# State-space stage on one core: VectorE takes x times dt ahead of two taps and of y's remainder, GpSimd the decayed x ahead of the gate weights' split

## Chip, cores and metric

One core of a Trainium2 chip runs the whole program. The metric is the device time of one execution in microseconds; three executions of the kernel before took 2430.52 to 2433.77 us, median 2432.82.

## What is computed

A network of two layers on 2 sequences of 512 tokens with 512 features: a Mamba2 mixer, a sparse dequantised linear layer, attention, and a gated feed-forward layer, each with a residual and a layer norm. The change lies in the mixer. Cut to what matters (128 heads of 64 channels in 8 groups, a state of 128, chunks of 128 tokens):

```python
xBC = silu(conv(xBC, conv_w, 4 taps) + conv_b)
x, Bm, Cm = split(xBC)
dt = clip(softplus(dt + dt_bias)); dA = dt * A; cs = cumsum(dA)      # per chunk
xdt    = x * dt
Ydiag  = (C B^T * exp(cs_l - cs_s), lower triangle) @ xdt
states = B^T @ (exp(cs_last - cs) * xdt)                              # per chunk
Yoff   = C @ previous_states * exp(cs)
y      = Ydiag + Yoff + x * D
yg     = y * silu(gate)
out    = (yg * rsqrt(mean(yg^2 over the group) + eps) * norm_w) @ out_proj_w.T
```

## The kernel before

The mixer works in 128 slots, one for each tile of 128 channels (two heads) of one sequence: 8 groups (g), in each 2 sequences (b) of 8 tiles (i). Channels lie on partitions and the sequence's 512 tokens in the free dimension, except behind the transposes of x, where tokens of a chunk lie on partitions. Slot n of all engines does these parts of neighbouring tiles, and each engine has its own written-out order of them:

- TensorE (from `scan` to `output`): the scan of tile n (lines 811 and 815, needs the masked E, the decayed C and the silu of the gate), the states of n+1 (lines 59 to 61, need the low half `xwlo` of the decayed x), the projection of x for n+3, that of the gate for n+1, the transposes of x of n+2 (`turn_x`, line 833), in some slots the projections, products or transposes of B and C for the next sequence, and the output projection of n-1. A projection is 12 matmuls of 512 columns: each fp32 operand is split in a leading 16-bit part and a remainder, and three products are summed.
- ScalarE: in every second slot the exps of n+1 and n+2 (line 996), then square and leading part of y (1002, 1005), in the first 8 slots of a group a copy of the output weights' leading part (230), tap 0 of x for n+3 (243), the clips of the decays for n+3 (990), the silu of the gate for n+1 (1009), the silu of x for n+3 (248), which waits for the third tap on VectorE.
- VectorE: u = x D + scan's bank of n (1176), the state recurrence of n+1 (1115, 1120), u times the gate's silu (1181), the mask on E of n+1 (1109), then the taps 1, 2 and 3 of x for n+3 (256) with y's remainder (1199) behind tap 1 and x times dt of n+2 (`turned_x`, 1128, reads the bank of the transposes) behind tap 2. In the first slot of each sequence four additions of the outputs (1148) follow, in two slots three taps of B or C.
- GpSimd: the decayed C of n+1 (`decayed_C`, 1280), the output weights' remainder (226), the sum of squares (1297), the remainders of the next group's weights (209: B, C, then x in slots 7 to 14, then the gate in slots 9 to 16), and the decayed x of n+2 (`decayed_x`: 1285 and its low half 1289), which waits for x times dt.
- SyncE issues the loads in a fixed order, each held by a semaphore: the rows of exp(cs) once the scan is done, those of cs once the clips that used their buffer are done, then weights.

Slots 1 to 16 are the body of a loop that runs 7 times (`slots`, line 676 on), slot 0 stands before it and 15 slots behind it. The slot that ends the body is the first of the next group, so each engine jumps back there six times between two bodies.

Of the kernel before, what the change touches and what calls it, by code (L numbers as in the profile page):

```python
# [33 lines left out]
def lead(words):  # L34

    return words.bitcast(BF16)[..., 1::2]
# [33 lines left out]
def tile_at(g, m):  # L70

    if isinstance(g, int) and not 0 <= 16 * g + m <= LAST_TILE:
        return None
    gg, mm = g + m // 16, m % 16
    return Tile(g * 16 + m, gg, mm // 8, mm % 8, gg * 2 + mm // 8)
# [13 lines left out]
def conv_of_slot(s, kind):  # L89
    if kind == "x":  # L90
        return s.u * 10 + (5 + (s.i if is_last_unit(s) else CONV_X[s.i]))
    return s.u * 10 + (5 + (CONV_B if kind == "B" else CONV_C))
# [20 lines left out]
def ring_bank(b, use):  # L113
    return (b + use) % 2
# [516 lines left out]
def mixer(k, io, sc, aw):  # L631
# [3 lines left out]
    with ExitStack() as tmp:  # L635
# [50 lines left out]
        def of_heads(table, t, c0, c1):  # L686

            return (table[:, CH * t.b + c0:CH * t.b + c1, bass.ds(t.g, 1), 2 * t.i:2 * t.i + 2].squeeze(2)
                    .unsqueeze(3).to_broadcast([P, c1 - c0, 2, HD]))

        def by_head(x):
            return x.rearrange("p c (h d) -> p c h d", d=HD)

        def chan(table, t):

            return table[:, bass.ds(t.g, 1), t.b, t.i:t.i + 1].squeeze(1)
# [5 lines left out]
        def next_unit(s):  # L702

            return None if is_last_unit(s) else Tile(s.u * 8 + 8, s.g + s.b, 1 - s.b, 0, s.u + 1)

        with nc.Block() as block:
# [397 lines left out]
            def _(dve):  # L1104
                def masked(t):
                    dve.wait_ge(exp_done, t.n + 1)
                    dve.wait_ge(cbm_done, t.u + 1)
                    e = E[t.i % 4][:].rearrange("p h c t -> p h (c t)")
                    nc.vector.tensor_tensor(e, e, cbm[t.b][:].rearrange("p c t -> p (c t)").unsqueeze(1).to_broadcast([P, 2, T]),  # L1109
                                            ALU.mult).then_inc(m_done, 1)  # L1110

                def state(t, c):
                    if c == 0:
                        dve.wait_ge(st_ready, t.n + 1)
                        nc.vector.tensor_copy(st[t.i % 2][:, 0], W[:, 0:P]).then_inc(s_step, 1)
                        return
                    dve.wait_ge(s_step, 3 * t.n + c)
                    for h in range(2):
                        r = slice(h * HD, (h + 1) * HD)
                        mm = nc.vector.scalar_tensor_tensor(  # L1120
                            out=st[t.i % 2][:, c, r], in0=st[t.i % 2][:, c - 1, r], scalar=head(sc.cd, t, c, h),
                            in1=W[:, c * P + h * HD:c * P + (h + 1) * HD], op0=ALU.mult, op1=ALU.add)
                    mm.then_inc(s_step, 1)

                def turned_x(t):

                    dve.wait_ge(xt_ready, t.n + 1)
                    nc.vector.tensor_tensor(by_head(xt[t.i % 2][:]), by_head(W[:, :].rearrange("p (c d) -> p c d", d=P)),  # L1128
                                            of_heads(sc.dtt, t, 0, CH), ALU.mult).then_inc(xt_done, 1)
# [11 lines left out]
                def mean_square(units, b):  # L1141
                    dve.wait_ge(ss_ready, units)
                    nc.vector.tensor_scalar(ms[:], bank_SS(units, b)[:, 0:CH], SPREAD ** 2 / GC, EPS * SPREAD ** 2,
                                            ALU.mult, ALU.add).then_inc(ms_done, 1)
# [26 lines left out]
                def slot(g, m):  # L1171
                    s, n1, n2, n3 = (tile_at(g, m + d) for d in range(4))
                    nu = next_unit(s)
                    ended = s.i == 0 and not (isinstance(s.u, int) and s.u == 0)
                    dve.wait_ge(y_ready, s.n + 1)
                    nc.vector.scalar_tensor_tensor(out=u[s.i % 2][:], in0=sc.xc[s.i % 4][:], scalar=chan(sc.D, s), in1=Y[:, :],  # L1176
                                                   op0=ALU.mult, op1=ALU.add).then_inc(y_done, 1)
                    if n1:
                        state(n1, 0)
                    dve.wait_ge(y_done, s.n + 1)  # L1180
                    nc.vector.tensor_tensor(u[s.i % 2][:], u[s.i % 2][:], gz[s.i % 2][:], ALU.mult).then_inc(yg_done, 1)  # L1181
                    if n1:
                        state(n1, 1)
                        state(n1, 2)
                        masked(n1)
                    if ended:
                        mean_square(s.u, s.b)

                    def taps(kind, dst, t, j, behind=(None, None)):
                        q = conv_of_slot(s, kind)  # L1190
                        bank = ring_bank(s.b, x_use(s) if kind == "x" else USE_B if kind == "B" else USE_C)
                        for d in range(1, 4):
                            sc.conv(dve, q, bank, dst, t.g, t.b, j, d)
                            if d < 3 and behind[d - 1]:
                                behind[d - 1]()

                    def remainder():
                        dve.wait_ge(hi_done, s.n + 1)
                        nc.vector.scalar_tensor_tensor(out=ylo[s.i % 2][:], in0=u[s.i % 2][:], scalar=chan(sc.nw, s),
                                                       in1=yhi[s.i % 2][:], op0=ALU.mult, op1=ALU.subtract).then_inc(lo_done, 1)  # L1200

                    if n3:
                        taps("x", sc.xc[n3.i % 4], n3, 2 + n3.i, (remainder, lambda: turned_x(n2)))
                    else:
                        remainder()
                        if n2:
                            turned_x(n2)
                    if nu and s.i == 2:
                        taps("B", sc.xcB, nu, 0)
                    if nu and s.i == 4:  # L1210
                        taps("C", sc.xcC[nu.b], nu, 1)
                    if nu and s.i == 5:
                        masked_CB(nu, ring_bank(s.b, USE_CB))
                    if nu and s.i == 6:
                        rest_of_B(nu, k.bank[ring_bank(s.b, USE_BT)])
                    if ended:
                        for half in range(2):
                            add_output(s.u, 1 - s.b, half)
                    if is_last_unit(s):
                        tail(s)  # L1220
# [54 lines left out]
            def _(pool):  # L1275
# [7 lines left out]
                def decayed_x(t):  # L1283
                    pool.wait_ge(xt_done, t.n + 1)
                    nc.gpsimd.tensor_tensor(by_head(xw[t.i % 2][:]), by_head(xt[t.i % 2][:, 0:CH - 1]), of_heads(sc.wdec, t, 0, CH - 1),  # L1285
                                            ALU.mult).then_inc(xw_done, 1)
                    pool.wait_ge(xw_done, t.n + 1)
                    x = xw[t.i % 2][:]
                    nc.gpsimd.tensor_tensor(xwlo[t.i % 2][:], x, lead(x), ALU.subtract).then_inc(xw_lo, 1)
# [21 lines left out]
                def slot(g, m):  # L1311
                    s, mm = tile_at(g, m), m % 16
                    more = not (isinstance(s.g, int) and s.g == NG - 1)
                    if tile_at(g, m + 1):
                        decayed_C(tile_at(g, m + 1))
                    if mm < XT:
                        sc.split_wo(pool, s.g, mm)
                    accumulate(s)
                    if s.i == 0 and not (isinstance(s.u, int) and s.u == 0):
                        root(s.u)  # L1320
                    if more:
                        if mm == 4:
                            sc.split_bc(pool, s.g + 1, 0)
                        if mm == 6:
                            sc.split_bc(pool, s.g + 1, 1)
                        if 7 <= mm <= 14:
                            sc.split_wx(pool, s.g + 1, mm - 7)
                        if 9 <= mm:
                            sc.split_wz(pool, s.g + 1, mm - 9)
                    if m == 16:  # L1330
                        sc.split_wz(pool, s.g, XT - 1)
                    if tile_at(g, m + 2):
                        decayed_x(tile_at(g, m + 2))
                    if is_last_unit(s):
                        tail(s)

# [1031 lines left out]
```

## Time and profile before

| | before |
|---|---|
| median of 3 runs | 2432.82 us (2430.52 to 2433.77) |
| the profiled execution | 2433.26 us |
| its span, first to last instruction | 2431.4 us |
| mean granted TensorE clock | 0.987 |
| TensorE matmuls busy | 2343.2 us (96%) |
| VectorE busy | 1794.1 us (74%) |
| ScalarE busy | 1584.3 us (65%) |
| GpSimd busy | 1377.3 us (57%) |

Groups are counted from 0, and so are the slots of a group (m). The state-space stage lasts from about 59 us to about 1510 us. Busy shares are means over all stages. A time-ordered row has a start, a duration, the engine, the line and the operation with the tile it writes and those it reads; brackets hold the idle time in front of it and what ended that. "issue" there is time in which the engine waited for nothing that the profile shows.

### The profile page before, as it was taken

Reading aid. Unit: us, or ns where it says so; the run is one execution under the profiler, and the core shown is the slowest. Engines: PE = TensorE matmul, PEld = TensorE weight load, DVE = VectorE, ACT = ScalarE, POOL = GpSimd, SP = SyncE. Lnnn points to the kernel's source line nnn. Section 1 sums busy time; section 2 is a strip of 40 time slices with the busy share of each in tenths; the row PEclk is TensorE's granted clock in tenths of the full one; section 3 lists DMA queues with packets and bytes.
Section 4 is the critical chain, followed back from the end, with each engine's and each line's share of the span. In section 5 each row is a group of like instructions: output and inputs, shape, how many; then the busy total and the mean of one; then the engine's idle time right before and its main releaser. Section 6 shows DMA issues by size and latency. Waiting matters only on the chain. (4 is left out here: it accounts for less than half of the span.)

```text
span 2431.4 us, 49850 instructions
## 1 busy us (share of the span) xinstructions
PE 2343.2 (96%) x16008; PEld 1328.4 (55%) x16008; DVE 1794.1 (74%) x3250; ACT 1584.3 (65%) x3327; POOL 1377.3 (57%) x1178
## 2 busy tenths in 40 slices
PE   6999999999999999999999998879999999999898
PEld 3555555555555555555555554445555556555444
DVE  6777777777777787777777885567787777888613
ACT  6776776776776776776776774355665555655533
POOL 5576576576576576576576579344344434454323
PEclk8999999999999999999999999889999999999999
DMA  7343343343343343343343441320010110100000
GB/s 244 120 134 113 111 136 113 112 137 111 111 137 111 110 136 113 112 137 111 112 137 110 132 152 36 129 89 14 36 40 14 41 36 14 40 10 14 1 1 35
DMA packets 117294, 218.95 MB, mean 90 GB/s; under 512 B 10016, under 2 KB 43424, under 8 KB 115840
## 3 DMA queue, kind: packets, MB, share of 16 engines
q1 hardware_dynamic: 116992, 215.29, 27.0%
q8 instruction: 145, 2.38, 0.4%
q14 instruction: 157, 1.29, 0.2%
HBM read 212.10 MB, written 3.15 MB: 89 GB/s over the span
## 5 line engine op out<-in xcount | busy, mean ns | idle before, releaser
L990 ACT ACTIVATE E<-wq,cst 128x128 f32<-128x128 f32 x1024 | 311.7, 389 | 2.2 <-PEq L298 2.2
L256 DVE SCALAR_TENSOR_TENSOR xc<-bank,taps,xc 128x511 f32<-128x511 f32 (+2 forms) x384 | 283.0, 737 | 24.6 <-ACT xc L243 24.1
L1963 POOL TENSOR_TENSOR qT<-qT,qrot 128x512 f32<-128x512 f32 x64 | 81.3, 1270 | 358.3 <-DVE qrot L1852 358.3
L1297 POOL TENSOR_TENSOR acc<-acc,sq 128x512 f32<-128x512 f32 x112 | 162.6, 1452 | 183.5 <-ACT sq L1002 183.5
L61 PE MATMUL bank<-xhi,wx 128*128 128x512 f16 x640 | 242.7, 379 | 0.0
L60 PE MATMUL bank<-xlo,wx 128*128 128x512 f16 x640 | 242.6, 379 | 0.0
L59 PE MATMUL bank<-xhi,wx 128*128 128x512 f16 x640 | 242.5, 379 | 0.0
L1109 DVE TENSOR_TENSOR E<-E,cbm 128x1024 f32<-128x1024 f32 x128 | 235.0, 1836 | 0.9
L1280 POOL TENSOR_TENSOR ecs<-ecs,xcC 128x768 f32<-128x768 f32 x128 | 235.2, 1837 | 0.4 <-POOLq L298 0.4
L1176 DVE SCALAR_TENSOR_TENSOR u<-xc,D,bank 128x512 f32<-128x512 f32 x128 | 95.7, 747 | 177.1 <-PE bank L815 166.4
L1285 POOL TENSOR_TENSOR xw<-xt,wdec 128x384 f32<-128x384 f32 x128 | 106.5, 832 | 174.5 <-DVE xt L1128 174.4
L811 PE MATMUL bank<-E,xt 128*64 128x128 f32 x2048 | 185.6, 280 | 14.6 <-issue 7.3
L1002 ACT ACTIVATE sq<-u 128x512 f32<-128x512 f32 x112 | 70.5, 629 | 196.8 <-DVE u L1181 195.5
L59 PE MATMUL bank<-xhi,wz 128*128 128x512 f16 x512 | 195.3, 381 | 0.4 <-DVE u L1176 0.3
L60 PE MATMUL bank<-xlo,wz 128*128 128x512 f16 x512 | 195.2, 381 | 0.0
L61 PE MATMUL bank<-xhi,wz 128*128 128x512 f16 x512 | 195.1, 381 | 0.0
L59 PE MATMUL bank<-wohi,yhi 128*128 128x512 bf16 x512 | 194.2, 379 | 0.0
L60 PE MATMUL bank<-wolo,yhi 128*128 128x512 f16 x512 | 194.2, 379 | 0.0
L61 PE MATMUL bank<-wohi,ylo 128*128 128x512 bf16 x512 | 194.2, 379 | 0.0
L1780 ACT ACTIVATE probs<-bank,nmx 128x512 f32<-128x512 f32 (+3 forms) x256 | 131.5, 526 | 67.6 <-DVE nmx L1882 67.6
L811 PEld LDWEIGHTS bank<-E,xt 128*64 128x64 f32 x2048 | 120.2, 137 | 64.6 <-issue 62.1
L209 POOL TENSOR_TENSOR wx<-wx 128x512 f16<-128x512 f32 x80 | 147.7, 1850 | 10.5 <-DMA wx<-in_w_xbc 10.5
(265 smaller groups left out, 6617.3 us busy)
## 6 DMA issues: line engine op xcount, KB each, us to landing
wq<-cs_rows SPq DMA_DIRECT2D x128, 512.0 KB, 4.0
ecs<-ecs_rows SPq DMA_DIRECT2D x128, 384.0 KB, 3.6
wx<-in_w_xbc SPq DMA_DIRECT2D x80, 256.0 KB, 2.6
wz<-in_w_z SPq DMA_DIRECT2D x64, 256.0 KB, 2.6
wo<-in_w_o SPq DMA_DIRECT2D x64, 256.0 KB, 3.9
wq<-in_wq SPq DMA_DIRECT2D x8, 1024.0 KB, 5.6
awo_raw<-in_wo SPq DMA_DIRECT2D x32, 256.0 KB, 3.0
wkv<-in_wkv SPq DMA_DIRECT2D x8, 512.0 KB, 3.7
```

Of the source, the lines that this page charges most:

```text
L59: nc.tensor.matmul(out, lhs[0], rhs[0], start=first, stop=False, skip_group_check=skip)
L60: nc.tensor.matmul(out, lhs[0], rhs[1], start=False, stop=False, skip_group_check=skip)
L61: return nc.tensor.matmul(out, lhs[1], rhs[0], start=False, stop=last, skip_group_check=skip)
L209: self.nc.gpsimd.tensor_tensor(rest(w), w, lead(w), ALU.subtract).then_inc(sem, 1)
L256: self.nc.vector.scalar_tensor_tensor(out=dst[:, d:T], in0=self.k.bank[bank][:, 0:T - d], scalar=self.taps[:, bass.ds(g, 1), b, j, 3 - d:4 ...
L811: mm = nc.tensor.matmul(Y[r, cols], xt[t.i % 2][:, c, r], E[t.i % 4][:, h, c], start=True, stop=c == 0, skip_group_check=True)
L990: ins = nc.scalar.activation(E[t.i % 4][:, h, c], sc.csr[t.i % 2][:, h, c * P:(c + 1) * P], ACT.Relu, scale=-1.0, bias=head(sc.cst, t, c, h))
L1109: nc.vector.tensor_tensor(e, e, cbm[t.b][:].rearrange("p c t -> p (c t)").unsqueeze(1).to_broadcast([P, 2, T]), ALU.mult).then_inc(m_done, 1)
L1280: nc.gpsimd.tensor_tensor(e[:], e[:], sc.xcC[t.b][:, P:T].unsqueeze(1).to_broadcast([P, 2, T - P]), ALU.mult).then_inc(cs_done, 1)
L1285: nc.gpsimd.tensor_tensor(by_head(xw[t.i % 2][:]), by_head(xt[t.i % 2][:, 0:CH - 1]), of_heads(sc.wdec, t, 0, CH - 1), ALU.mult).then_inc( ...
L1297: nc.gpsimd.tensor_tensor(acc[t.b][:], acc[t.b][:], sq[:], ALU.add).then_inc(acc_done, 1)
L1780: ins = nc.scalar.activation(pr[h % 2][:, P_OFF[i]:P_OFF[i] + (i + 1) * P], k.bank[bank][:, at:at + (i + 1) * P], ACT.Exp, bias=nmx[h % 2] ...
```

## The change

Two moves, with no operation added or removed. On VectorE the two pieces behind the taps of x change places: x times dt of tile n+2 comes behind tap 1, y's remainder of tile n behind tap 2. On GpSimd the decayed x of n+2 comes ahead of the split of the next group's gate weights, in slots 9 to 16; in the other slots there is no such split and the order is as before. In the last group GpSimd's order does not change.

```diff
@@ vector, slot
                     if n3:
-                        taps("x", sc.xc[n3.i % 4], n3, 2 + n3.i, (remainder, lambda: turned_x(n2)))
+                        taps("x", sc.xc[n3.i % 4], n3, 2 + n3.i, (lambda: turned_x(n2), remainder))
@@ gpsimd, slot
                             sc.split_bc(pool, s.g + 1, 1)
                         if 7 <= mm <= 14:
                             sc.split_wx(pool, s.g + 1, mm - 7)
-                        if 9 <= mm:
-                            sc.split_wz(pool, s.g + 1, mm - 9)
+                    if tile_at(g, m + 2):
+                        decayed_x(tile_at(g, m + 2))
+                    if more and 9 <= mm:
+                        sc.split_wz(pool, s.g + 1, mm - 9)
                     if m == 16:
                         sc.split_wz(pool, s.g, XT - 1)
-                    if tile_at(g, m + 2):
-                        decayed_x(tile_at(g, m + 2))
```

## Rows read from the trace of the kernel before

**Rows 1.** Busy time of each engine in three stretches, with clock and DMA share

```profile
core 0: us, PE busy (x) PEld busy (x) DVE busy (x) ACT busy (x) POOL busy (x), PEclk, DMA share, GB/s
100.00:1430.00 1330.00, 1325.10 (x9635) 750.59 (x9634) 1028.99 (x1708) 976.45 (x1888) 870.05 (x669) 1.00 0.38 121
...
425.40:447.43 22.03, 21.43 (x163) 11.89 (x161) 17.05 (x32) 15.33 (x32) 12.27 (x12) 1.00 0.27 95
607.63:629.94 22.31, 21.41 (x163) 11.89 (x161) 17.85 (x32) 15.33 (x32) 12.21 (x12) 1.00 0.27 93
```

**Rows 2.** The waits from 100 to 1430 us: total, times, longest

```profile
POOL xw L1285 <- DVE xt L1128: 154.8, 117, 3.8
DVE u L1176 <- PE bank L815: 152.7, 108, 2.9
...
PEld bank L811 <- issue: 47.6, 102, 1.1
...
DVE u L1176 <- issue: 10.6, 6, 2.1
...
PEld bank L59 <- POOL xwlo L1289: 2.0, 6, 0.3
```

**Rows 3.** Time-ordered rows of a plain slot with a gate split, from 408 us

```profile
408.63 0.74 DVE L256 SCALAR_TENSOR_TENSOR xc<-bank,taps,xc 128x511 f32<-128x511 f32 x1
...
409.29 0.86 DVE L1199 SCALAR_TENSOR_TENSOR ylo<-u,nw,yhi 128x512 f16<-128x512 f32 x1
...
409.57 0.60 PE L833 MATMUL bank<-identity,xc 128*128 128x128 f32 x4
409.57 1.49 POOL L209 TENSOR_TENSOR wz<-wz 128x512 f16<-128x512 f32 x1
...
410.08 0.74 DVE L256 SCALAR_TENSOR_TENSOR xc<-bank,taps,xc 128x510 f32<-128x510 f32 x1
...
410.74 0.68 DVE L1128 TENSOR_TENSOR xt<-bank,dtt 128x512 f32<-128x512 f32 x1
...
411.33 0.73 DVE L256 SCALAR_TENSOR_TENSOR xc<-bank,taps,xc 128x509 f32<-128x509 f32 x1
...
411.59 0.83 POOL L1285 TENSOR_TENSOR xw<-xt,wdec 128x384 f32<-128x384 f32 x1 [0.53 <-DVE xt L1128]
...
412.50 0.83 POOL L1289 TENSOR_TENSOR xwlo<-xw 128x384 f16<-128x384 f32 x1
```

**Rows 4.** Time-ordered rows of loop ends, engine by engine

```profile
424.89 2.00 ACT L996 ACTIVATE E<-E 128x1024 f32<-128x1024 f32 x2
...
428.87 0.78 ACT L243 ACTIVATE xc<-bank,taps 128x512 f32<-128x512 f32 x1
...
448.03 2.00 ACT L996 ACTIVATE E<-E 128x1024 f32<-128x1024 f32 x2
...
451.58 0.77 ACT L243 ACTIVATE xc<-bank,taps 128x512 f32<-128x512 f32 x1
...
1158.64 0.77 ACT L243 ACTIVATE xc<-bank,taps 128x512 f32<-128x512 f32 x1
...
430.23 1.05 POOL L209 TENSOR_TENSOR wz<-wz 128x512 f16<-128x512 f32 x1
...
432.21 0.37 SPq L197 DMA_DIRECT2D wq<-cs_rows  x1
...
425.40 0.75 DVE L1176 SCALAR_TENSOR_TENSOR u<-xc,D,bank 128x512 f32<-128x512 f32 x1 [2.49 <-PE bank L815]
...
430.45 1.36 DVE L1199 SCALAR_TENSOR_TENSOR ylo<-u,nw,yhi 128x512 f16<-128x512 f32 x1
...
433.65 2.71 DVE L1148 SCALAR_TENSOR_TENSOR resid<-bank,rstd,resid 128x512 f32<-128x512 f32 x4
438.48 0.75 DVE L1176 SCALAR_TENSOR_TENSOR u<-xc,D,bank 128x512 f32<-128x512 f32 x1 [2.12 <-issue]
...
1154.55 0.75 DVE L1176 SCALAR_TENSOR_TENSOR u<-xc,D,bank 128x512 f32<-128x512 f32 x1 [2.49 <-PE bank L815]
...
1167.73 0.75 DVE L1176 SCALAR_TENSOR_TENSOR u<-xc,D,bank 128x512 f32<-128x512 f32 x1 [1.38 <-issue]
```

**Rows 5.** The gate's silu and the scan behind it in the ninth slot of group 2

```profile
524.89 0.60 ACT L1009 ACTIVATE gz<-bank 128x512 f32<-128x512 f32 x1
...
525.82 0.42 PEld L811 LDWEIGHTS bank<-E,xt 128*64 128x64 f32 x8 [0.42 <-issue]
```

## The prediction

> **What bounds the kernel now.** I read the page's busy shares first, then the stage as one window, then the table of waits of the stage, then a plain slot and a loop end in time order. TensorE is busy 96% of the span, and between 100 and 1430 us, nearly all of the stage that the change touches, 1325 of 1330 us [rows 1]. So a slot lasts as long as its matmuls, and a reordering on VectorE or GpSimd can only give back what is left of TensorE's idle time, or add to it. The table of waits says how little that is: 2.0 us in six waits for the low half of the decayed x, which is exactly what the change hurries, and behind it 47.6 us in 102 pieces ahead of a scan, about 0.42 us each, which stand in plain slots too where nothing is late [rows 2]. GpSimd, on the other hand, waits 154.8 us for VectorE's turned x, and VectorE 152.7 us for the scan's bank [rows 2]. Both are slack, since nobody on TensorE waits for them in a plain slot.
>
> **The plain slot, step by step [rows 3].** Today VectorE runs tap 1 at 408.63, y's remainder at 409.29, tap 2 at 410.08, x times dt at 410.74, tap 3 at 411.33 to 412.06. With the change x times dt stands behind tap 1, which ends at 409.37. TensorE's transposes of that x run only from 409.57 to 410.17. A signal between engines takes about 0.17 us (x times dt ends at 411.42, GpSimd begins at 411.59), so x times dt can begin at about 410.34: 0.40 us earlier than now, after 0.97 us of new waiting. Behind it wait tap 2, the remainder and tap 3, by name.
> Tap 2 then begins 0.60 us later, at 410.94, and the remainder would at 411.60. There it meets the decayed x, which GpSimd begins at 411.19 (the 0.40 earlier) and ends at 412.02. What such a meeting costs is shown at 430.45, where the remainder takes 1.36 us: the split that GpSimd began at 430.23 ends at 431.28, and the remainder 0.53 us behind it; the one at 409.29 took 0.86 [rows 3, 4]. So the remainder ends at about 412.6, the low half, due at 412.1, waits for it and ends at 413.4, against 413.33 now, and tap 3 runs from 412.55 to 413.28: **1.22 us later**. The 0.40 us won on x times dt is given back by the collision. Bounds: without the collision tap 3 is 0.8 us later and the low half 0.4 us earlier; with a remainder that must let the low half go first too (0.83 us), tap 3 is some 2.0 us later.
> The Trainium skill (GPSIMD Engine Reference, Key points) says that GpSimd shares its SBUF interfaces with VectorE and contends with VectorE instructions that have two SBUF inputs; the remainder has two, and the 1.36 us row agrees. Without that rule the low half would be 0.4 us earlier in each plain slot, still with nobody waiting for it.
>
> **GpSimd's half of the change.** In slots 9 to 15 of a group the gate weights' split (1.05 us alone, 1.49 beside the remainder [rows 3, 4]) now runs behind the decayed x. It filled GpSimd's wait for VectorE; that wait becomes longer and the split comes after. No matmul of this group reads it (it is a gate weight of the next one), no load is held on it. What it pushes is the next slot's decayed C, by about 1.1 us, which the scan reads a whole slot later. It costs VectorE up to 0.6 us in the product with the gate, where a short slot follows; in an even slot that product is not what ScalarE waits for, as next shown. I cost it at nothing on TensorE; the cover is that slot's length, and gone it would be the 0.6 us.
>
> **What is late next: ScalarE.** Its silu waits for tap 3, then comes a table load, and in every second slot the pair of exps, the square, and the tap of the next x. At the loop end of group 1 the exps end at 426.89 and the tap begins at 428.87 [rows 4]. Where ScalarE ran without a gap, the tap began 1.55 us behind the exps (450.03 to 451.58 [rows 4]). With tap 3 late by 1.2 the exps end at about 428.1 and the tap begins at 429.65: 0.78 us later. Who waits for it? Two places.
> (a) The ninth slot (m = 8) of a group. The gate's silu ends at 525.49 and the scan begins at 525.82 [rows 5]. Its tap moves by about 0.2 us (no output weight to copy there, 0.6 us less), the silu ends at 525.7, plus 0.12: just inside. Cost 0; if tap 3 is 0.3 us later still, 0.3 in each of 8 slots.
> (b) The loop end. VectorE's last addition ends at 436.36, and its next instruction comes only at 438.48, 2.12 us later, on "issue" [rows 4]; six such gaps make 10.6 us [rows 2]. In that slot pair TensorE is idle for 0.6 us (21.43 busy of 22.03), in group 2's for 0.9 [rows 1]. The restart is 9.61 us behind ScalarE's tap in group 1, and 9.09 in group 5 (1158.64 to 1167.73), while from the last addition it varies more. I read it so: the clips behind the tap release SyncE's row load (432.21), a burst of data follows, and VectorE's code for the next pass comes behind that burst. So the restart moves with the tap. New tap 4.25 us behind the slot's u; today 3.47 in group 1 and 4.09 in group 5 [rows 4]; of the six, two are like the first and four between. Shifts 0.78 and 0.16, mean about 0.45, times 6: **+2.7 us**. Bounds: 0 (the restart has its own time), 0.78 x 6 = 4.7.
> Advanced Engine Details and Errata of the Trainium skill (Control Flow Timing) gives a taken branch about 51 ns. The 2.12 us row says otherwise here; by the page VectorE would restart with the last addition, the rival below.
> (c) The gain: at the six loop ends TensorE waits 0.3 us for the low half [rows 2]. VectorE is late there and the transposes are done before it asks, so x times dt begins two instructions earlier, 2 x 0.66 us (410.08 to 410.74 from start to start [rows 3]), and the low half, after the collision, about 0.9 earlier. About 0.17 of the 0.33 is the ordinary gap between a scan and the states behind it; the rest goes: 0.17 x 6 = **-1.0 us**.
> First slots and the last group's end, where GpSimd is full, I put at +0.2, within 0.6 either way.
>
> **Sum:** 2.7 - 1.0 + 0.2 = +1.9 us on the profiled execution's 2433.26, that is 2435.2. Its span is 2431.40, with 1.9 us around it, and it lies 0.44 above the median of the three runs, 2432.82; so 2434.7 for the median. That is no change within 0.2% (4.9 us), about what a measurement here can tell.
>
> **Rivals.**
> - *ScalarE becomes the bound (slower).* Place: tap 3, silu, exps, tap, clips, silu of the gate, scan. Point: it decides once tap 3 is over some 1.3 us late, as with the remainder losing to both GpSimd products (2.0 us). Then the ninth slots lose about 0.6 x 8 = 5 us, the loop ends 2.7 + 0.7 x 6 = 7, less 1.0: 2444; half of that delay gives 2 + 4.8 - 1.0, 2439. Against it: every other even slot is longer. 0.14.
> - *VectorE restarts behind its last addition (a small loss).* Tap 3 is followed by four additions (433.65, 2.71 us); 1.1 us later in group 1, about 0.6 in the mean, times 6: +3.7 in place of 2.7, 2435.7. Against it: the restart varies by more from there. 0.12, inside 0.2%.
> - *The wait that goes is all there is to see.* The restart has its own time: -1.0 + 0.2, 2432.0. 0.18, inside 0.2%.
> - *Faster beyond 0.2%.* All that TensorE loses at the six loop ends vanishes, up to 0.9 us each: 2427.4. Nothing in the rows frees the 2.12 us. 0.05.
> - My forecast: 0.51.
>
> **How the numbers follow.** Of one sign or nearly nothing: 0.51 + 0.12 + 0.18 = 0.81 within 0.2%; 0.14 slower and 0.05 faster. The range runs from below the third rival (2430.5) to the half-way case of the first (2439.5).
>
> **What would show it.** Right: x times dt begins some 0.75 us behind the start of its transposes in every plain slot, with VectorE idle before it; remainders longer than now; tap 3 about 1.2 us later; VectorE's wait for the scan's bank down by about as much per slot; GpSimd's wait for the turned x no smaller; TensorE's six waits for the low half gone; slots of the same lengths to 0.01 us but at loop ends. Wrong: plain slots longer, "gz" as releaser of the scan in ninth slots, or loop ends moved by more than 0.8 us.

## The result, and the profile after

The changed kernel takes 2441.77 us (median of 11 runs, 2436.82 to 2447.11), the kernel before beside it 2433.77 (11 runs, 2430.52 to 2438.87). The ratio is 1.003, with a 95% interval of 1.002 to 1.004: **about 8 us slower**, outside the 0.2% that I had called no change and above my range. The profiled execution took 2442.54 us, with a span of 2440.7.

What I had described in the plain slot happened nearly row for row. These are the time-ordered rows of the changed kernel in the slot that answers to [rows 3], up to the load of the next slot's states:

```profile
409.98 0.74 DVE L256 SCALAR_TENSOR_TENSOR xc<-bank,taps,xc 128x511 f32<-128x511 f32 x1
...
410.87 0.60 PE L833 MATMUL bank<-identity,xc 128*128 128x128 f32 x4
...
411.61 0.69 DVE L1128 TENSOR_TENSOR xt<-bank,dtt 128x512 f32<-128x512 f32 x1 [0.90 <-PE bank L833]
...
412.22 0.74 DVE L256 SCALAR_TENSOR_TENSOR xc<-bank,taps,xc 128x510 f32<-128x510 f32 x1
...
412.57 0.83 POOL L1285 TENSOR_TENSOR xw<-xt,wdec 128x384 f32<-128x384 f32 x1 [1.61 <-DVE xt L1128]
...
412.88 1.07 DVE L1199 SCALAR_TENSOR_TENSOR ylo<-u,nw,yhi 128x512 f16<-128x512 f32 x1
...
413.48 1.15 POOL L1289 TENSOR_TENSOR xwlo<-xw 128x384 f16<-128x384 f32 x1
...
413.87 0.73 DVE L256 SCALAR_TENSOR_TENSOR xc<-bank,taps,xc 128x509 f32<-128x509 f32 x1
...
414.64 0.63 ACT L248 ACTIVATE xc<-xc 128x512 f32<-128x512 f32 x1 [0.99 <-DVE xc L256]
...
415.18 0.46 ACT L1013 CAST bthi<-bank 128x384 f16<-128x384 f32 x1
...
415.67 0.56 DVE L1138 TENSOR_TENSOR btlo<-bank,bthi 128x384 f16<-128x384 f32 x1 [1.06 <-ACT bthi L1013]
...
416.28 0.10 PEld L59 LDWEIGHTS bank<-xw,bthi 128*128 128x128 f16 x1 [0.46 <-DVE btlo L1138]
```

x times dt begins 0.74 us behind the start of the transposes. The remainder meets the decayed x and ends 0.55 us behind it (413.95 against 413.40). Tap 3 starts 3.89 us behind tap 1 (413.87 less 409.98), against 2.70 in [rows 3] (411.33 less 408.63): 1.19 us late, where I had 1.22. The last three rows are what I had not looked at. This is the seventh slot of a sequence (i = 6), and in it ScalarE makes the leading part of the turned B (`bthi`) *behind* the silu of x, so behind tap 3, and VectorE its remainder (`btlo`) behind that. TensorE's states of the next sequence's first tile read both, and wait. The same three operations before:

```profile
412.77 0.47 ACT L1013 CAST bthi<-bank 128x384 f16<-128x384 f32 x1
...
413.27 0.56 DVE L1138 TENSOR_TENSOR btlo<-bank,bthi 128x384 f16<-128x384 f32 x1 [1.21 <-ACT bthi L1013]
...
414.69 0.10 PEld L59 LDWEIGHTS bank<-xw,bthi 128*128 128x128 f16 x1 [0.17 <-issue]
```

B's remainder was done at 413.83, 0.86 us before the states began: that was the room. Now it ends 1.92 us behind the scan's first load (416.23 and 414.31), where it was 0.82 (413.83 and 413.01): 1.10 us later. The load follows its end by 0.05, so 0.81 of the 1.10 is room and 0.29 is paid by TensorE.

The waits of TensorE and the ones that I had forecast, after, from 100 to 1430 us (total, times, longest; answers to [rows 2]):

```profile
POOL xw L1285 <- DVE xt L1128: 154.6, 113, 3.4
ACT xc L248 <- DVE xc L256: 143.4, 101, 2.3
...
DVE xt L1128 <- PE bank L833: 80.7, 94, 1.4
DVE u L1176 <- PE bank L815: 72.1, 60, 1.5
PEld bank L811 <- issue: 49.0, 101, 1.1
...
DVE u L1176 <- issue: 9.6, 6, 2.1
...
PEld bank L59 <- DVE btlo L1138: 3.4, 7, 0.7
PE bank L59 <- DVE btlo L1138: 3.3, 14, 0.4
```

The row of the low half (2.0 us in six) is gone, as forecast, and two rows that name `btlo` stand in its place. The new wait of VectorE for the transposes is 80.7 us, and its wait for the scan's bank fell by 80.6: the step within VectorE is free, the one through ScalarE is not.

How long slots last, from VectorE's u of one slot to that of the next, is read best from sums of windows. Slots 7 and 15 of all groups, in which those states are made (15 of them), before:

```profile
sum 157.33, PE 157.33 PEld 88.72 DVE 120.31 ACT 109.83 POOL 119.77; mean PE 10.49 PEld 5.91 DVE 8.02 ACT 7.32 POOL 7.98
```

and after:

```profile
sum 161.43, PE 159.63 PEld 92.08 DVE 125.70 ACT 95.52 POOL 121.81; mean PE 10.64 PEld 6.14 DVE 8.38 ACT 6.37 POOL 8.12
```

That is +4.10 us, 0.27 in each. (The busy time of PE is no measure here: the trace of after lacks some matmul records.) The six loop ends come next: slots 0 and 1 together of groups 1 to 6. A loop end is named after the group that ends there, so the one of group 1 is slots 0 and 1 of group 2, at 425 us ([rows 1] show those of groups 1 and 2). Before:

```profile
242.74:265.19 22.45, 21.39 (x163) 11.88 (x161) 17.98 (x31) 15.31 (x32) 12.19 (x12) 1.00 0.29 90
...
sum 132.92, PE 128.01 PEld 71.46 DVE 106.10 ACT 91.94 POOL 73.39; mean PE 21.34 PEld 11.91 DVE 17.68 ACT 15.32 POOL 12.23
```

and after:

```profile
243.91:266.38 22.47, 21.40 (x164) 12.04 (x164) 17.46 (x31) 16.11 (x33) 15.14 (x12) 1.00 0.31 92
426.99:450.07 23.08, 21.41 (x164) 12.06 (x164) 17.46 (x32) 16.12 (x33) 15.18 (x12) 1.00 0.28 90
...
sum 135.11, PE 128.04 PEld 72.38 DVE 104.75 ACT 96.62 POOL 90.97; mean PE 21.34 PEld 12.06 DVE 17.46 ACT 16.10 POOL 15.16
```

That is +2.19, very uneven: 1.05 and 1.03 at the ends of groups 1 and 4, 0.18 at that of group 5, nothing at the other three. The sum itself repeats: the three runs below that keep VectorE's new order in these slots have 135.08, 135.78 and 136.01.

Slot by slot, the whole stage from u of slot 0 to u of slot 120 went from 1368.28 to 1375.08 us, +6.80, and it adds up: slots 7 and 15 +4.10; loop ends +2.19; the first two slots of group 0 +1.0 (u of slot 0 itself came 0.4 earlier) and of group 7 +0.5; slots 2 and 3 behind a loop end -0.96 (23.77 to 23.61 in each of six). What is left comes to under 0.1 us in sum. Slots 8 and 9 have to be taken together: slot 8, with its four additions, is 1.18 longer, and slot 9 is 1.18 shorter (21.21 for the two, before and after). A few other neighbours shift between one another in the same way.

Slots 120 to 126, the last, add 1.76 us (83.51 and 85.27). Of these 0.3 lie in the slots of the last sequence up to 125, and 1.45 in slot 126 alone (10.90 and 12.35). That one is not the reordering's: it lasts 12.26 us in late_tap and 12.40 in rem_last_old, described below, and 10.90 in dve_half, which has the same order there as the changed kernel. Behind the stage the code is the same, and its length differs from one profile to the next of any kernel here (732.1 us before, 734.5 after, 730.7 to 734.4 in others, for the stretch from attention's first exps to the first silu of the feed-forward layer). So the profiled pair's 9.3 us is a few more than the change made, and the median's 8 is the number to explain; some 7 of it are found here.

### The profile page after: what moved, and what is told of

It reads as the page before. It is cut to its first block and busy times, and to the rows that moved or that the text cites. A ratio compares the mean times of both kernels' runs of the same rounds, so it can differ in the third digit from the quotient of the medians.

```text
span 2440.7 us, 49653 instructions
## 1 busy us (share of the span) xinstructions
PE 2335.9 (96%) x15811; PEld 1330.9 (55%) x16008; DVE 1802.4 (74%) x3250; ACT 1579.0 (65%) x3327; POOL 1381.9 (57%) x1178
## 5 line engine op out<-in xcount | busy, mean ns | idle before, releaser
L1297 POOL TENSOR_TENSOR acc<-acc,sq 128x512 f32<-128x512 f32 x112 | 172.7, 1542 | 168.5 <-ACT sq L1002 168.5
L1109 DVE TENSOR_TENSOR E<-E,cbm 128x1024 f32<-128x1024 f32 x128 | 222.4, 1737 | 1.1 <-ACT E L996 0.2
L248 ACT ACTIVATE xc<-xc 128x512 f32<-128x512 f32 x128 | 80.5, 630 | 151.8 <-DVE xc L256 151.8
L1128 DVE TENSOR_TENSOR xt<-bank,dtt 128x512 f32<-128x512 f32 x128 | 88.2, 689 | 91.6 <-PE bank L833 91.3
```

The lines of the kernel that those rows point to most:

```text
L1297: nc.gpsimd.tensor_tensor(acc[t.b][:], acc[t.b][:], sq[:], ALU.add).then_inc(acc_done, 1)
```

## Experiments

Ratios are to the kernel before, in runs on the same chip, with 95% intervals. Profiles are of one execution each; a sum of loop ends from one is good to about 1 us (135.08 to 136.01 for the same order), and worse where the granted clock falls (rem_last_new).

**dve_half** has VectorE's half of the change alone.

```diff
-  taps(..., (remainder, lambda: turned_x(n2)))
+  taps(..., (lambda: turned_x(n2), remainder))
```

> Only VectorE's half: x times dt behind tap 1, y's remainder behind tap 2; GpSimd's order as before. My theory: the loss is all VectorE's. Tap 3 ends about 1.2 us later, ScalarE's silu and its copy of the transposed B behind it too, and VectorE's low half of B comes late for the states of the next sequence's first tile: 15 slots (the eighth and the last of each group) with about 0.28 us each, 4.2 us; loop ends 2.2 us, last group 2 us, start 0.6 us, less 1.0 us for the low half of x: +7 to +9 us against the kernel before, the slots at the loop ends within 0.3 us of the whole change's. Rival, the loss is GpSimd's (the split behind the decayed x pushes the decayed C into VectorE's product with the gate): at most +4 us here, and slots 7 and 15 as long as before, 10.49 us.

2439.89 us, 1.0024 [1.0014, 1.0033], about +5.8. Slots 7 and 15 take 160.77 us (+3.4), the loop ends 135.08 (+2.2), and TensorE waits for `btlo` as after (4.2 us against 6.7). This half carries most of the loss.

**pool_half** has GpSimd's half alone (decayed x ahead of the split of the gate weights).

> Only GpSimd's half: the decayed x ahead of the gate weights' split; VectorE's order as before. My theory: x times dt still comes last, the decayed x starts when it did (7.5 us into a slot), the split behind it pushes the decayed C of the next slot by about 1 us; VectorE's product with the gate is blocked by up to 0.7 us where the slot before was short. At the loop ends of groups 1 and 4 ScalarE's tap moves by up to 0.6 us and the restart with it: 0 to +1.5 us in all, no wait for the low half of B. Rival: +4 us or more, slots 7 and 15 longer.

2436.91 us, 1.0008 [0.9998, 1.0018]. The interval holds no change; the profile has +2.95 at the loop ends and no change in slots 7 to 15. These are its time-ordered rows at group 1's loop end:

```profile
426.55 1.83 POOL L1280 TENSOR_TENSOR ecs<-ecs,xcC 128x768 f32<-128x768 f32 x1
...
427.41 1.52 DVE L1181 TENSOR_TENSOR u<-u,gz 128x512 f32<-128x512 f32 x1
...
428.96 0.63 ACT L1002 ACTIVATE acc<-u 128x512 f32<-128x512 f32 x1 [0.65 <-DVE u L1181]
...
430.62 0.77 ACT L243 ACTIVATE xc<-bank,taps 128x512 f32<-128x512 f32 x1
```

The split pushes the decayed C beside VectorE's product with the gate, which takes 1.52 us instead of 0.68, and here ScalarE's square does wait for it (0.65). The tap starts 4.07 us behind the slot's u (3.47 in [rows 4]). I had named that 0.6 us and costed it at nothing "in an even slot", looking only at slots in which the exps end later. The two halves do not add up: in the changed kernel the exps end at 429.63, later than that product (427.86 and 1.14 us), and hide it. VectorE's restart behind the six turns does not follow its last addition here: in the mean that ends 0.47 us earlier than before, and the restart comes 0.49 later, with a tap 0.30 later.

**after_b_first** is the changed kernel, with ScalarE's leading part of the turned B ahead of the silu of x.

```diff
@@ scalar, slot
+  if nu and s.i == 6:
+      turned_B(nu, k.bank[ring_bank(s.b, USE_BT)])
...
-  if nu and s.i == 6:
-      turned_B(nu, k.bank[ring_bank(s.b, USE_BT)])
```

> The changed kernel, with ScalarE's copy of the transposed B ahead of the silu of x in the seventh slot of each sequence, so that it no longer stands behind tap 3. My theory: VectorE's low half of B comes right behind tap 3, TensorE's wait for it (6.7 us in the two rows) is gone, slots 7 and 15 are 10.49 us again: +3.5 to +5 us against the kernel before, in place of +8. Rival, that slots 7 and 15 are long because the silu and the exps are late on ScalarE: they stay 10.77 us, +8.

2438.85 us, 1.0016 [1.0005, 1.0027]. No engine waits for `btlo`, and slots 7 and 15 are back:

```profile
sum 157.36, PE 156.57 PEld 88.74 DVE 126.57 ACT 95.20 POOL 121.68; mean PE 10.44 PEld 5.92 DVE 8.44 ACT 6.35 POOL 8.11
```

4.07 us less than in the changed kernel by the profiles, 3.4 by the ratios (0.0014 of 2434, though the intervals overlap). This is the direct test of the missed path. Some 4 us remain, which are the loop ends and the start.

**after_last_old** is the changed kernel, with VectorE's old order in the last sequence alone.

```diff
-  (lambda: turned_x(n2), remainder)
+  (remainder, lambda: turned_x(n2)) if is_last_unit(s) else (lambda: turned_x(n2), remainder)
```

> The changed kernel, with the old order on VectorE in the last sequence alone, where GpSimd has the linear layer's weights to make and is full. My theory: the stage's end is lost there, 2.0 us of the difference arises behind slot 120: +5.5 to +6.5 us against the kernel before. Rival, it is the clock or the states of the transposes there: no difference to the changed kernel, +8.

2440.80 us, 1.0027 [1.0018, 1.0037]: under 1 us less than the changed kernel, which the intervals can't tell from none. In its profile slots 120 to 126 take 83.55 us (85.27 in the changed kernel), but 1.45 of that is slot 126, which varies by itself. What the order does in the last sequence is 0.3 us.

**slot1_only** is the kernel before, with VectorE's new order only behind the loop's turn, where the wait for the low half was.

```diff
+  (lambda: turned_x(n2), remainder) if m % 16 == 1 else (remainder, lambda: turned_x(n2))
```

> The kernel before, with VectorE's new order (x times dt ahead of tap 2 and the remainder) in one slot of sixteen only, the second of each group, behind the loop's turn; GpSimd as before. Theory (the wait of TensorE for the low half behind a loop end is the one thing that the change can give back, and what it costs elsewhere is not in this slot): those waits, 2.0 us in six, go and nothing takes their place, so 0.5 to 1.5 us less than before; slots 0 and 1 of groups 1 to 6 together as before, slots 2 and 3 shorter by about 0.16 us in each group. Rival (the later tap 3 of this slot is paid for at once, ScalarE being late behind a loop end): 0 to 1.5 us more than before, by 0.2 us in each group.

2432.39 us, 0.9993 [0.9984, 1.0003]. Slots 2 and 3 take 23.61 (23.77 before) and slots 0 and 1 132.11 over six (132.92). So the gain that the change could bring is there, about 1 us, and too small to be told in the times.

**rem_last_old** is the kernel before, with y's remainder behind tap 3 and x times dt kept behind tap 2.

```diff
-  taps(..., (remainder, lambda: turned_x(n2)))
+  taps(..., (None, lambda: turned_x(n2)))
+  remainder()
```

> The kernel before, with VectorE's order tap 1, tap 2, x times dt, tap 3, remainder: the remainder moves behind tap 3, GpSimd as before. Theory (in the changed kernel tap 3 is late by the wait for the transposes and by the meeting of the remainder with the decayed x, and what costs time is tap 3's lateness, through B's halves and the silu): here tap 3 starts about 0.4 us earlier than in the kernel before, B's halves too, and slots 7 and 15 last 10.49 us as before; total within 1 us of the kernel before, or 1 to 2 us less if the loop's restart follows ScalarE's tap. Rival (it is the remainder that counts: its product is read by TensorE, and now comes over 2 us later): TensorE waits for it in nearly every slot, and the total is over 5 us more.

2429.61 us, 0.9981 [0.9972, 0.9990]: **4.6 us faster than before**, more than the theory gave. In the slot of [rows 3]:

```profile
409.64 0.69 DVE L1128 TENSOR_TENSOR xt<-bank,dtt 128x512 f32<-128x512 f32 x1
...
410.25 0.73 DVE L256 SCALAR_TENSOR_TENSOR xc<-bank,taps,xc 128x509 f32<-128x509 f32 x1
...
410.50 0.83 POOL L1286 TENSOR_TENSOR xw<-xt,wdec 128x384 f32<-128x384 f32 x1 [0.57 <-DVE xt L1128]
...
410.90 0.98 DVE L1199 SCALAR_TENSOR_TENSOR ylo<-u,nw,yhi 128x512 f16<-128x512 f32 x1
...
412.59 0.56 DVE L1138 TENSOR_TENSOR btlo<-bank,bthi 128x384 f16<-128x384 f32 x1 [0.71 <-ACT bthi L1013]
```

The remainder meets the decayed x here too (0.98 us), but nobody waits for it. Slots 7 and 15 stay at 157.35 over 15, the loop ends take 131.42 over six (-1.5), slots 2 and 3 23.68. The profile accounts for 2.2 us of the stage, the ratio's interval begins at 2.4. The profiled execution (2433.12) was the slowest of its 11, 3.5 us above their median, so it is no good witness for the rest, which stays open. The rival (TensorE waits for the remainder) is out.

**rem_last_new** has x times dt behind tap 1, as the change, and the remainder behind tap 3.

```diff
+  taps(..., (lambda: turned_x(n2), None))
+  remainder()
```

> The kernel before, with VectorE's order tap 1, x times dt, tap 2, tap 3, remainder: the wait for the transposes stays as in the changed kernel, the meeting with the decayed x moves behind tap 3. Theory: tap 3 starts about 0.06 us earlier or later than in the kernel before (0.97 us of wait in place of the remainder's 0.79), so B's halves are in time, slots 7 and 15 last 10.49 to 10.55 us, and the total is within 1.5 us of the kernel before, not 5 us above it as with VectorE's half of the change. Rival (the wait itself costs: two engines are in step now and lose time in every slot, whoever stands behind): the total is 4 to 7 us above the kernel before, as with VectorE's half.

2432.31 us, 0.9993 [0.9984, 1.0002], so the wait for the transposes does not cost by itself. Slots 7 and 15 take 157.33. I had put tap 3 within 0.06 us of before; its two last taps end at 414.01, 0.46 us ahead of the scan's load (412.06 and 413.01 before: 0.95), so it is 0.49 late, inside the 0.81 of room. Its profile is of its slowest execution (2438.83, 6.5 above the median) and has two loop ends of 24.8 us, those of groups 0 and 2, where no other profile here has one over 23.3. In both TensorE starts the scan of slot 1, the first thing behind its own turn, after 2.4 us in which it waited for nothing that the profile shows, and then its granted clock is 1.2 GHz for 3.41 us:

```profile
252.79 0.66 PEld L811 LDWEIGHTS bank<-E,xt 128*64 128x64 f32 x8 [2.40 <-issue]
...
252.96:256.37 3.41, 3.41 (x33) 3.08 (x33) 1.49 (x3) 0.00 (x0) 1.34 (x2) 0.50 0.08 23
621.60:625.01 3.41, 3.41 (x29) 2.64 (x26) 1.88 (x4) 0.00 (x0) 1.04 (x1) 0.50 0.05 13
```

(The column of the clock reads 0.50.) No other profile here has a low clock at a loop end. Slot 1 is 1.75 and 2.35 us longer there than its usual 8.94, and 3.41 us at half the clock are an estimated 1.7 us of work lost. What held TensorE for the 2.4 us is not shown.

**late_tap** is the kernel before, with one spare square ahead of ScalarE's leading part in slot 16.

```diff
+  if m == 16:
+      act.wait_ge(spare_done, s.g)
+      nc.scalar.activation(spare[:], u[s.i % 2][:], ACT.Square).then_inc(spare_done, 1)
```

> The kernel before, with one spare square of a 128x512 tile (about 0.5 to 0.6 us) on ScalarE ahead of its leading part of the last slot of a group, so that ScalarE's tap of that slot, and the clips and SyncE's row load behind it, come later by that much; VectorE's own work is unchanged. It is done eight times. Theory (VectorE's restart behind a loop end follows ScalarE's tap): VectorE's first instruction behind the loop's turn is about 0.5 us later at each of the six loop ends, slots 0 and 1 of groups 1 to 6 together are longer by 0.2 to 0.5 us each, total 1.5 to 3 us more. Rival (the restart has its own time, or follows VectorE's last addition): slots 0 and 1 unchanged to 0.1 us, total within 0.7 us of the kernel before.

2436.34 us, 1.0014 [1.0005, 1.0023], about +3.4. The tap moved by only 0.27 us in the mean of six (part of the square filled idle time), the restart by 0.41, the loop ends by 2.46 in sum, though VectorE's last addition ended 0.16 *earlier*. The rival, that the restart has its own time or follows the last addition, falls. What the spare square moves is the tap, the clips behind it and with them both loads that SyncE issues there; the run does not tell these apart.

**rows_after_jump** is the kernel before, with SyncE's load of the rows of cs in the loop's last slot written one slot later, behind the turn.

```diff
@@ sync, slot
+  if m % 16 == 1:
+      sc.hold(sp, clip_done, tile_at(g, m - 1).n + 4)
+      sc.load_csr(sp, tile_at(g, m + 4))
...
-  if t:
+  if t and m % 16:
```

> The kernel before, with only SyncE's row load of the slot at the loop's end issued one slot later, behind the loop's turn. Theory: restart earlier at six loop ends, slots 0 and 1 of groups 1 to 6 together shorter by 1.5 to 4 us over the six, total 1.5 to 4 us less. Rival (the load is not what the restart follows): slots 0 and 1 together within 0.7 us of the kernel before over six, total within 1 us.

2429.14 us, 0.9978 [0.9969, 0.9987]: **5.4 us faster than before**. The six loop ends (compare the sum of 132.92):

```profile
241.54:263.45 21.91, 21.20 (x164) 12.11 (x164) 18.05 (x32) 15.51 (x32) 12.39 (x12) 1.00 0.32 96
...
sum 129.93, PE 126.98 PEld 72.13 DVE 105.92 ACT 92.64 POOL 73.88; mean PE 21.16 PEld 12.02 DVE 17.65 ACT 15.44 POOL 12.31
```

and VectorE's restart in group 1, behind its four additions:

```profile
432.32 2.71 DVE L1151 SCALAR_TENSOR_TENSOR resid<-bank,rstd,resid 128x512 f32<-128x512 f32 x4
436.37 0.75 DVE L1179 SCALAR_TENSOR_TENSOR u<-xc,D,bank 128x512 f32<-128x512 f32 x1 [1.33 <-issue]
```

With the same tap (3.76 us behind u in the mean, 3.80 before) and the same additions, the restart comes 12.60 us behind u instead of 13.21.

What the edit moved in time is not what it, or the expectation, says. Behind the turn the row load waits for the same clips as ahead of it, so it is issued when it was: 7.16 us behind u in the mean, 7.14 before. But behind it in SyncE's order stood a load of 256 KB, the output weights of the next slot (`wo`), which now need not wait for the clips. Before it is issued right behind the row load (432.21 in [rows 4]), here right at the slot's start, at u 423.47:

```profile
432.90 0.34 SPq L192 DMA_DIRECT2D wo<-in_w_o  x1
```

```profile
424.43 0.35 SPq L192 DMA_DIRECT2D wo<-in_w_o  x1
430.71 0.38 SPq L197 DMA_DIRECT2D wq<-cs_rows  x1
```

In the mean of six it went from 7.83 to 0.96 us behind u. SyncE also makes its own turn without waiting for the clips, and the packet records have two packets of code at 3.3 and 5.6 us behind u that were not there before. So the run shows that the restart hangs on what SyncE has in front of its turn. Whether it is the 256 KB less in the burst, or SyncE's earlier turn, it does not tell.

**rlo_rows** puts the last winner and rem_last_old together.

> VectorE's order tap 1, tap 2, x times dt, tap 3, remainder (as in the run of that order), and besides SyncE's row load of the slot at the loop's end is issued one slot later, behind the loop's turn. Theory (VectorE's code for the next pass comes behind the burst of data that this load adds to; the run with the late tap showed the restart to follow the tap): with less data ahead of the code VectorE restarts up to 1 us earlier at each of six loop ends, slots 0 and 1 of groups 1 to 6 together 21.2 to 21.7 us each, total 1 to 3 us less than that order alone, which is 2426 to 2429. Rival (the other data of the burst, or the code's own time, sets the restart): slots 0 and 1 as with that order alone (131.4 us over six), total within 1 us of it.

2428.89 us, 0.9983 [0.9974, 0.9992]. The profile has the loop ends that were expected (129.51 over six, 21.5 to 21.8 each) and the shortest stage of all (1362.09 us to slot 120); the times don't show it ahead of either part alone. Their intervals overlap almost wholly, so whether the two add up is not settled.

**rlo_pool** is rem_last_old with GpSimd's half of the change.

> VectorE's order tap 1, tap 2, x times dt, tap 3, remainder together with GpSimd's half of the change (the decayed x ahead of the gate weights' split). Theory (GpSimd's half costs only at the loop ends and at the start, as its run alone showed by some 2 us; in other slots the split has room): slots 7 and 15 last 10.49 us, slots 8 and 9 together 21.21, total 1 to 3 us above that VectorE order alone, so 2431 to 2433. Rival (with the remainder behind tap 3 the split meets it and both end later, TensorE or ScalarE waits): slots 4 to 14 longer than before by over 0.05 us each, total over 4 us above that order alone.

2428.50 us, 0.9983 [0.9974, 0.9992]. Loop ends 130.95, slots 7 and 15 at 10.49, 8 and 9 at 21.21. GpSimd's half shows no cost here, less than the theory's 1 to 3 us, though each ratio is good to 2 us only.

**all3** has the three together.

> All three together: VectorE's order tap 1, tap 2, x times dt, tap 3, remainder; SyncE's row load of the slot at the loop's end one slot later; and GpSimd's half of the change. Theory (the first two each end TensorE's loop-end waits, GpSimd's half costs nothing once tap 3 is early): slots 0 and 1 of groups 1 to 6 together 129 to 130 us, total within 1 us of the version without GpSimd's half, so 2426 to 2429. Rival (GpSimd's half keeps its own price of about 2 us, hidden so far behind the loop ends): slots 0 and 1 together 131 us or more, total 2430 or more.

2431.18 us beside 2434.25, 0.9985 [0.9976, 0.9994]; loop ends 130.71. No better than with fewer parts. The five kernels with the remainder behind tap 3 and x times dt in its old place, or with the edit of rows_after_jump, or both, are all faster than the two kernels compared, and can't be told from one another.

## Why the prediction was wrong, by its own steps

- **The plain slot** was right, but for slots 7 and 15: 0.74 us for x times dt behind the transposes' start (0.77 by my numbers), tap 3 1.19 us late (1.22), the low half no earlier, the others unchanged. (That the slots keep their lengths one by one, as I had written, fails for slots 8 and 9, which exchange 1.18 us.) The Trainium skill (GPSIMD Engine Reference, Key points) has GpSimd's contention with VectorE instructions of two SBUF inputs; the remainder's 1.07 us here agrees.
- **The step that failed** is the one on "What is late next: ScalarE", at "Who waits for it? Two places." There was a third. I followed the silu of x to the exps and the next tap, but not the other operation that ScalarE has behind that silu in every eighth slot: the leading part of the turned B, with VectorE's remainder behind it and TensorE's states behind both. Its room was 0.81 us, and the delay 1.10. It cost 0.27 in each of 15 slots, 4.1 us, a term that the sum did not have; after_b_first takes it away by moving that one operation and gives the 4.1 back. In the waits of before nobody waits for `btlo`, so nothing there says how near it was: a table of waits shows who is late, not who is nearly late. But VectorE's own wait in front of it stood there, once for each of those 15 slots, and would have led me to the chain:

```profile
DVE btlo L1138 <- ACT bthi L1013: 18.2, 15, 1.3
```

- **(a) Ninth slots**, costed 0: 21.21 us for slots 8 and 9 together, before and after. Right, and by its mechanism: the gate's silu ends 8.67 us behind u in place of 8.49, and the scan begins at 8.81 in both.
- **(b) Loop ends**, +2.7: measured +2.19, the tap 0.38 us later in the mean (0.45 by me) and the restart 0.37. That the restart does not follow the rival's last addition is shown by late_tap and pool_half, and that it hangs on SyncE's loads or its turn by rows_after_jump. But the near agreement of the sum is in part luck. I had the shift of the restart equal to that of the tap at each loop end. At the ends of groups 1 and 4 the tap came 0.72 later and the restart 1.05 and 1.03; at the ends of 0, 2 and 3 it came 0.24, 0.35 and 0.17 later and the restart not at all. With all six taps at 4.18 the restarts lie between 13.22 and 14.13 us behind u. So the tap is one term of several, and the reading that the row load is what it acts through was not tested as I meant. The Trainium skill (Advanced Engine Details and Errata, Control Flow Timing) has a branch that is always taken at about 51 ns and a compare-and-branch at about 108. VectorE's idle time at group 1's turn is 1.33 us in rows_after_jump and 2.12 in [rows 4], so here something other than the branch's own time is paid.
- **(c) The low half**, -1.0: measured -0.96. Right.
- **GpSimd's half**, 0: about right in the changed kernel, but only because the later exps hide it. Its one trace there is in slots 15, 10.78 us after against 10.69 in dve_half, 0.6 us over seven. Alone it has 2.95 us at the loop ends in its profile, by the product that I had named and in a slot where I had ruled it out.
- **Start and end**, +0.2 within 0.6: the first slots of group 0 and of group 7 have +1.0 and +0.5. Under-sized, if they are the change's. The first is not shown to be: late_tap, whose code there is that of the kernel before, has 24.55 us in the first two slots, more than the changed kernel's 24.39 (23.40 before). I did not trace them further.
- **The rivals.** The slower one had the right sign, and its 2439 to 2444 hold the result. But its place, ninth slots through the gate's silu, is where no time was lost, and its point (a remainder that lets GpSimd go twice, 2.0 us) was not reached. I argued that nobody on TensorE waits in a plain slot, and the very slot that I read in [rows 3] has the turned B in it: its two operations (412.77 and 413.27) stand right behind tap 3, and I followed that tap only to the silu.

## What to carry to other kernels

Where an order is written out by hand and differs by slot, follow a delayed operation through *every* kind of slot: list what each engine has queued behind it, and for each item the room between its end and its reader's start. Moving a piece of work that nobody waits for (y's remainder) behind one that many wait for (tap 3) was worth 4 us here; the change moved a wait ahead of that tap, to hurry something that was late in six slots of 128. And what an issuing engine has in front of a loop's turn can delay another engine's start behind it. When a load is moved in a fixed order, look up in the trace when each load behind it was issued: the one that moved in time may be another.

## What the hardware showed that I had not expected

- VectorE's restart behind a loop's turn hangs on what SyncE does in front of it. From ScalarE's tap to the restart it is 9.1 to 9.6 us in the six turns before. It stays 9.0 to 10.0 where VectorE's last addition ends 0.5 us later (the changed kernel) or 0.5 earlier (pool_half), and is 8.4 to 9.2 in rows_after_jump, with the 256 KB of output weights out of the burst and SyncE past its turn early. It is no fixed distance either (8.9 to 9.6 in rem_last_old, 9.2 to 10.3 in rem_last_new, whose last addition is 0.79 us later). In the packet records the turn's first three code packets of one queue have begun by 10.71 us behind the slot's u before (mean of six), as a burst of data ends, and by 10.20 in rows_after_jump (not counting the two at 3.3 and 5.6 us); the restart comes 0.61 earlier. That VectorE's code is among them and stands behind the data is a reading that fits; neither whose code they hold nor what delays them was tried.
- A meeting of VectorE's remainder with a GpSimd product ends about 0.55 us behind the GpSimd operation: 413.95 against 413.40 after, and 411.88 against 411.33 in rem_last_old. So its cost hangs on when the two start: 0.98, 1.07 and 1.36 us (the last in [rows 4]) for the same operation. The product with the gate in pool_half keeps the same distance: it ends at 428.93, behind the decayed C at 428.38.
